# Phase 2 of a transformer block: the statistics of the third layer norm in two halves, with the low halves of the attention rows between them on VectorE

## What is computed

```
u = layernorm(x)
y = u + linear_attention(layernorm(u, g1, b1)) @ wo         # 16 heads of 16
z = y + table_gelu(layernorm(y, g2, b2) @ w1) @ w2           # 256 -> 1024 -> 256, gelu read at steps of 0.1
p = x + z                                                    # the residual around the block
out = p + layernorm(p) @ CB.T * (SCB / 127) + bias
```

## Time and profile before

| | us |
|---|---|
| runs | 575.92, 574.35, 576.08 (median 575.92) |
| profiled execution, its own time | 573.73 |
| span of its trace | 571.9 |
| granted TensorE clock over the span | 0.990 of full speed |
| busy: PE 536.6, PEld 486.8, DVE 448.7, ACT 394.7, POOL 348.5 | |

### The profile page before, as it was taken

How to read it: one execution, slowest core, us unless ns; L and a number is a source line. 1 busy time by engine, 2 the same in 40 slices (tenths; PEclk the granted TensorE clock), 3 DMA queues, 4 the chain that set the end, 5 groups by cost and what they waited for, 6 DMA issues and landing times.

```text
span 571.9 us, 11318 instructions
## 1 busy us (share of the span) xinstructions
PE 536.6 (94%) x3610; PEld 486.8 (85%) x3610; DVE 448.7 (78%) x1059; ACT 394.7 (69%) x656; POOL 348.5 (61%) x336
## 2 busy tenths in 40 slices
PE   6799999999999899999999999999999999999895
PEld 6788888788887789889898898988989899898775
DVE  5789889789776587888878878787886978879636
ACT  2386785555567686877768787687876968768760
POOL 3343444325143467687877868768687786877654
PEclk9799998999999999999999999999999999999999
DMA  8421221121001010110102101021010101100001
GB/s 272 134 74 63 85 73 39 37 74 37 22 19 57 1 37 24 51 68 5 73 0 73 54 21 74 0 73 40 34 73 0 73 37 37 73 0 37 38 1 76
DMA packets 11419, 29.47 MB, mean 52 GB/s; under 512 B 2048, under 2 KB 4864, under 8 KB 11392
## 3 DMA queue, kind: packets, MB, share of 16 engines
q1 hardware_dynamic: 9472, 28.32, 13.6%
q10 hardware_dynamic: 1920, 0.79, 0.7%
HBM read 20.71 MB, written 8.39 MB: 51 GB/s over the span
## 4 chain that ended last, share of the span: by engine, by line
PE 59%; DVE 20%; issue 10%; ACT 5%; POOL 4%; DMA 2%; DVEq 0%; ACTq 0%; POOLq 0%; SPq 0%
PE psum L1028 54%; PE psum L1046 4%; DVE bn_stats_b L690 3%; DVE bn_stats L690 2%; DMA f_arena<-in_L_attn_x_dram 2%; DVE f32r_arena L843 2%; POOL f32r_arena L383 2%; DVE n_and_ones L717 2%; DVE f32r_arena L835 2%; DVE mean_var L697 1%; DVE phi_q L741 1%; ACT f_arena L501 1%; DVE f_arena L736 1%; ACT psum L524 1%; DVE f32r_arena L725 1%
## 5 line engine op out<-in xcount | busy, mean ns | idle before, releaser
L1028 PE MATMUL psum<-w_hi,f32r_arena 128*128 128x256 f32 x1280 | 174.3, 282 | 4.7 <-POOL f32r_arena L383 3.0
L1028 PEld LDWEIGHTS psum<-w_hi,f32r_arena 128*128 128x128 f32 x1280 | 164.0, 188 | 14.2 <-issue 5.9
L1028 PE MATMUL psum<-f32r_arena,w_hi 128*128 128x512 f32 x512 | 141.1, 403 | 0.8 <-issue 0.8
L383 POOL TENSOR_TENSOR f32r_arena<-f_arena,f32r_arena 128x512 fp32r<-128x512 f32 x64 | 85.9, 1343 | 82.1 <-ACT f32r_arena L620 46.0
L607 ACT ACTIVATE grid_index<-psum,w_bias_in_steps 128x512 int8<-128x512 f32 x128 | 87.0, 680 | 47.3 <-PE psum L1028 47.2
L1028 PEld LDWEIGHTS psum<-f32r_arena,w_hi 128*128 128x128 f32 x512 | 88.1, 188 | 14.2 <-issue 1.0
L618 ACT ACTIVATE f_arena<-grid_index 128x512 f32<-128x512 int8 x128 | 80.8, 632 | 24.9 <-POOL f32r_arena L383 16.5
L620 ACT ACTIVATE f32r_arena<-grid_index 128x512 fp32r<-128x512 int8 x128 | 79.2, 619 | 0.0
L1028 PE MATMUL psum<-f32r_arena 128*128 128x256 f32 (+1 forms) x384 | 68.0, 333 | 1.9 <-DVE f32r_arena L729 1.9
L1028 PEld LDWEIGHTS psum<-f32r_arena 128*128 128x128 f32 x384 | 58.3, 196 | 8.2 <-issue 2.1
L835 DVE TENSOR_TENSOR f32r_arena<-f_arena,f32r_arena 128x512 fp32r<-128x512 f32 x64 | 57.2, 893 | 3.0 <-ACT f32r_arena L620 3.0
(11 more groups left out here) (117 smaller groups left out, 874.5 us busy)
## 6 DMA issues: line engine op xcount, KB each, us to landing
f_arena<-in_L_attn_x_dram SPq DMA_DIRECT2D x32, 512.0 KB, 3.3
out_dram<-f_arena SPq DMA_DIRECT2D x15, 512.0 KB, 2.6
f_arena<-in_L_attn_w_dram SPq DMA_DIRECT2D x2, 1024.0 KB, 12.5
out_dram<-f_arena SPq DMA_DIRECT2D x2, 256.0 KB, 2.1
phi_q<-in_L_attn_wk_dram ACTq DMA_DIRECT2D x1, 256.0 KB, 4.5
phi_q<-in_L_attn_wq_dram SPq DMA_DIRECT2D x1, 256.0 KB, 4.7
phi_q<-in_L_ffn_CB_dram SPq DMA_DIRECT2D x1, 256.0 KB, 7.1
phi_q<-in_L_attn_wo_dram SPq DMA_DIRECT2D x1, 256.0 KB, 7.4
```

Source lines behind the costliest of these rows:

```text
L383: nc.gpsimd.tensor_tensor(t_lo[m % SLOTS], tf[m % 2], t_hi[m % SLOTS].bitcast(F32), ALU.subtract).then_inc(s["t_lo_p"], 1)
L1028: return nc.tensor.matmul(out_, lhs, rhs, start=start, stop=stop, skip_group_check=True)
```

## The change

On VectorE, the four `bn_stats` of xp are issued as two and two. Between the two pairs stand `attend(1, 1)` and low 1 (body 0 only, which has no predecessor) and `attn_low(i + 1)`. The four `bn_aggr`, which wait for `bn3`, follow the second pair, ahead of low 1. In bodies 0 and 15 the order of instructions stays as it was.

```diff
+            def half_sums3(h):
+                for j in (2 * h, 2 * h + 1):
+                    i = ve.bn_stats(bn_b[:, 6 * j:6 * j + 6], tm(xp)[:, j])
+                if h == 1:
+                    i.then_inc(s["bn3"], 1)
...
                 if prv:
                     v.wait_ge(s["xp_ready"], c + 1)
-                    sums(xp, bn_b, "bn3")
-                    mean_var(i - 1, bn_b, mv3, "bn3", "mv3_ready")
+                    half_sums3(0)
                 if is_chunk(i, 0):
                     attend(1, 1)
                     mlp_low(i, 1)
                 if nxt:
                     attn_low(i + 1)
+                if prv:
+                    half_sums3(1)
+                    mean_var(i - 1, bn_b, mv3, "bn3", "mv3_ready")
                 if is_chunk(i, 0):
                     turned_sums(1, SA)
                     mlp_low(i, 3)
                 else:
                     mlp_low(i, 1)
```

## The result

The changed kernel takes 590.79 us (median; 588.85 to 591.29), the kernel before beside it 575.13 (574.2 to 576.08): a ratio of 1.0261, 95% interval 1.0235 to 1.0287, or 15.7 us more. I had forecast 582.8, range 575.5 to 589. The sign was right, the size less than half of what came, and the time lies outside the range. The granted clock of the profiled executions is 0.991 of full speed here and 0.990 before, so it isn't the clock.

What follows compares the result with a forecast made beforehand. PE was taken to bound the kernel, with POOL close behind. 14 bodies x 0.49 = +6.9 us on the profiled 573.73 gave 580.6; with 2.19 from profiled run to median, 582.8, range 575.5 to 589.

Steps and rivals of the forecast that it cites:

- What goes: PE's wait for L843 vanishes; output product could start 0.63 to 0.78 us earlier per body, alone 8.8 to 10.9 gain.
- What is late instead: DVE to POOL: aggregates end 1.31 us later, first L362 starts 0.89 later, power and third norm 1.25 late.
- the 0.37 of the prediction: POOL's first L362 waits out low 1's L835 on DVE, adding 0.37 us at worst; the worst was taken.
- Followed through the body: Late third norm traced through the engines to down 7: each of 14 bodies grows by 0.49 us.
- CB product +0.38: On PE, the CB product waits for the late L847 pair and starts 0.38 us later.
- Low 5 and low 6: DVE's low 5 no longer meets POOL's low 6, which takes 1.30 us instead of 1.84; 0.54 comes back.
- Rival 1: Low 5 and low 6 still meet, low 7 0.54 us later, 1.03 a body, 590.3 us; chance 0.12.
- down 7 waits for low 7: At the body's end, POOL's low 7 ends at 346.02 and lets PE's down 7 start at 346.16; body +0.49 us.
- Rivals 2 and 3: 2: first L362 not held up, 577.6 us, chance 0.16. 3: POOL's chain does not decide, 567.1 us, chance 0.12.

Runs made afterwards that it cites:

- half of L401: Changed kernel with low 5 on GpSimd and low 6 on VectorE, bias addition L401 cut to two of a partition's four rows: 581.22 us, ratio 1.0083.

## Why the prediction was wrong

**What goes: right.** L843 ends 1.12 earlier in the body, ACT's high halves cover it, and PE no longer waits for it.

**What is late instead: right to 0.05 us.** The first L362 started 0.20 behind the aggregates instead of 0.09 and took 0.43 instead of 0.57 (behind low 1, as I had it); its end came out 0.02 off. The error in its start did not count, since its end is set by the end of low 1 (333.66, 0.05 ahead of it), as the prediction had it. But being held up cost less than the 0.37 of the prediction: from its later start of 333.28 it would have ended at 333.48 with 0.20, and ended at 333.71, 0.23 behind that.

**Followed through the body: here it failed.** I moved low 3's end to 13.82, which is what was measured, and used it only for the L847 pair behind it on VectorE. That down 3 also needs low 3 I left out, though the order on TensorE (down 2, up 5, down 3) puts it two groups behind down 2: down 3 could not start before 13.97 by my own numbers (13.82 and the release of 0.15; it started at 13.88), nor the CB product before about 15.9. The term "CB product +0.38" should have been +1.1 (measured 15.86 - 14.77 = 1.09). In the earlier trace rows low 3 ends at 334.16, and the row of down 3 (334.48) was the one not looked at. The runs show that it is this: up 6 ahead of down 3 alone takes the body from 25.10 to 24.56, and half of L401 from 25.11 to 24.44, where my forecast had 24.48 (23.99 + 0.49). With up 6 first the forecast's own path comes out too: the CB product follows the L847 pair, as far as its rows show, and low 7 ends 24.47 after the body's down 7 (24.43 forecast), 0.15 ahead of the next.

**Low 5 and low 6: wrong, as a consequence.** With the CB product late by 1.09, low 5 was late too and met low 6 (1.68). With up 6 first it is 1.30, as forecast. Rival 1 named this meeting and came near the time (590.3), but by the wrong mechanism, so its time was luck: taking the meeting away left the body at 25.11. The forecast's claim that down 7 waits for low 7 was wrong for the same cause: low 7 ended 0.37 ahead of it.

**Rivals 2 and 3: not so.** L362 was held up (0.43 instead of 0.20; the same in the bodies on either side), and GpSimd's lateness of 1.28 at its end reached the end of low 3 as 1.25 and down 3 as 0.99. 0.30 less at the aggregates made the body 0.29 shorter.

**The range.** It held bounds for costs I could not see (the L362 meeting) but none for a dependency left out; 589 fell 1.8 short. 351.4 - 335.8 = 15.6 against 14 x 0.49 = 6.9: 8.7 us were missing. Breaking this one link shortened the 14 bodies by 7.5 us (351.4 to 343.9, up 6 first) and by 9.3 (351.5 to 342.2, half of L401), one a little less than that and one a little more.

## What to carry to other kernels

When an operation is made late by a known amount, list every instruction that waits for each late result, on all engines, and not only the next one on its own queue; a result that was 0.3 us early for its reader stops being early when two engines slip together. Before moving work on the engine that feeds a wait, see if the waiting engine has work of its own to put there: here up 4 and up 6 at other places on TensorE, with one ScalarE step moved to suit, won 0.70 of the 0.78 us a body (0.78 with low 5 and low 6 exchanged as well), while moving the producer's work cost 1.11.

## What the runs showed of the hardware

In these traces an L835 on VectorE, which reads two tiles in SBUF, and an instruction of GpSimd that reads SBUF take turns. Low 3 ended 0.54 behind L401 in the changed kernel (340.67 and 340.13), and low 0 0.55 behind L417 where the bias was moved (334.08 and 333.53), so that an L835 of 0.68 took 1.34 and 1.92. With the L835 first it was GpSimd's small L362 that waited: it ended 0.05 behind low 1 (333.71 and 333.66) and took 0.43 instead of 0.20. That is the rule of the Trainium skill that the prediction cited (SBUF — State Buffer, "Who interferes with whom"), and these runs agree with it.

VectorE operations with one input in PSUM kept their time beside GpSimd's reads: all 15 xp additions took 1.22 to 1.23 in each kernel, and L857 1.22 with low 2 beside it.
